# A decoder block with routed experts on one core: the early tiles of the first expert hold tokens of four groups instead of six, and the narrowest up products have 224 columns instead of 256

## What is computed

```python
N, E, K, CF = 4096, 8, 2, 1.25
cap = int(N * K * CF / E)                       # 1280
logits = x @ Wg.T
top_v, top_i = jax.lax.top_k(logits, K)
gates = jax.nn.softmax(top_v, axis=-1)
...
keep = pos_f < cap                              # pos: the token's place in its expert's queue
exp_batches = zeros((E, cap, d)).at[flat_e, pos_safe].set(x[tok], mode='drop')
h = einsum('ecd,edf->ecf', exp_batches, W1)     # 512 -> 2 x 1024: "up"
inp, gate = split(h, 2, axis=-1)
h = gelu(inp, approximate=False) * gate
exp_out = einsum('eci,eid->ecd', h, W2)         # 1024 -> 512: "down"
out = segment_sum(gates * gathered rows of exp_out, tok)
```

## Time and profile before

| what | us |
|---|---|
| median of 3 runs (lowest to highest) | 1474.22 (1474.14 to 1477.27) |
| the profiled execution's own time | 1474.55 |
| its span, first to last instruction | 1472.8 |
| PE busy in the span | 1430.7 |
| first up product of the early tiles | at 472.37 |
| first up product of the first expert's later tokens | at 512.43 |

### The profile page before, as it was taken

The page is one execution under the profiler, slowest core; times in us unless marked ns, Lnnn a source line. Parts: engine busy times, 40 slices in busy tenths (PEclk is TensorE's granted clock), DMA queues, the critical chain, the costliest instruction groups (busy, mean ns, idle before and its releaser), DMA issues.

```text
span 1472.8 us, 22222 instructions
## 1 busy us (share of the span) xinstructions
PE 1430.7 (97%) x7508; PEld 1210.8 (82%) x7509; DVE 640.8 (44%) x1379; ACT 591.7 (40%) x1018; POOL 374.8 (25%) x365
## 2 busy tenths in 40 slices
PE   7999999989989999999999999999999999999997
PEld 5768887778876888889889888899889888898886
DVE  7535666657777563123524421166223420253111
ACT  5534554258776552223424421255323321252212
POOL 3302232137666412203202211121301111021111
PEclk9999999999998999999999999999999999999999
DMA  6331223218658764204505421156504412052112
GB/s 206 60 64 30 86 87 58 86 33 209 172 133 221 176 186 108 42 2 85 151 34 123 107 64 34 21 157 189 132 7 118 103 57 43 7 152 54 21 36 28
DMA packets 82854, 135.64 MB, mean 92 GB/s; under 512 B 33234, under 2 KB 33362, under 8 KB 81780
## 3 DMA queue, kind: packets, MB, share of 16 engines
q1 hardware_dynamic: 65428, 97.68, 23.2%
q0 software_dynamic: 17376, 37.30, 13.8%
HBM read 94.41 MB, written 40.55 MB: 92 GB/s over the span
## 4 chain that ended last, share of the span: by engine, by line
PE 90%; DVE 3%; ACT 2%; issue 2%; DMA 1%; POOL 1%; SPq 0%; POOLq 0%; DVEq 0%; ACTq 0%
PE pg L1050 16%; PE pg L1052 16%; PE pg L1051 16%; PE pj L1050 10%; PE pj L1051 10%; PE pj L1052 10%; PE pj L1289 2%; PE pg L1317 2%; PE pt L1458 2%; PE pg L1255 2%; PE pt L1276 1%; PE pt L1071 1%; DMA out_rows<-ost,etab 1%; DVE kf L1582 1%; PE pt L1201 1%
## 5 line engine op out<-in xcount | busy, mean ns | idle before, releaser
L1050 PE MATMUL pg<-xe_hi,w_hi 128*128 128x512 f32 (+2 forms) x1152 | 401.7, 349 | 3.0 <-DVE xe_lo L1534 1.9
L1051 PE MATMUL pg<-xe_lo,w_hi 128*128 128x512 f32 (+2 forms) x1152 | 401.1, 348 | 0.0
L1052 PE MATMUL pg<-xe_hi,w_lo 128*128 128x512 f32 (+2 forms) x1152 | 401.0, 348 | 0.0
L1994 DVE TENSOR_TENSOR hp<-gl,pg 128x512 f32<-128x512 f32 x136 | 93.5, 688 | 569.9 <-ACT gl L1021 569.9
L728 POOL DMA_INDIRECT out_rows<-ost,etab x62 | 99.6, 1606 | 721.7 <-ACT ost L1005 359.0
L1021 ACT ACTIVATE gl<-pg 128x512 f32<-128x512 f32 x136 | 81.3, 598 | 410.9 <-PE pg L1052 410.9
L1050 PEld LDWEIGHTS pg<-xe_hi,w_hi 128*128 128x128 f32 x1152 | 218.5, 190 | 29.0 <-issue 2.8
L1051 PEld LDWEIGHTS pg<-xe_lo,w_hi 128*128 128x128 f32 x1152 | 218.5, 190 | 25.0
L1052 PEld LDWEIGHTS pg<-xe_hi,w_lo 128*128 128x128 f32 x1152 | 218.5, 190 | 25.0
L1050 PE MATMUL pj<-w_hi,hg_hi 128*128 128x512 f32 x448 | 177.0, 395 | 0.0
L1052 PE MATMUL pj<-w_hi,hg_lo 128*128 128x512 f32 x448 | 174.5, 389 | 0.0
(11 more groups left out here) (250 smaller groups left out, 1992.8 us busy)
## 6 DMA issues: line engine op xcount, KB each, us to landing
stage<-w SPq DMA_DIRECT2D x96, 512.0 KB, 4.1
xr<-x SPq DMA_DIRECT2D x8, 1024.0 KB, 10.6
out_rows<-xr SPq DMA_DIRECT2D x8, 1024.0 KB, 7.3
x_rows<-xn SPq DMA_DIRECT2D x8, 1024.0 KB, 7.1
x_in<-x SPq DMA_DIRECT2D x7, 1024.0 KB, 6.0
x_rows<-zrow POOLq DMA_DIRECT2D x1, 2304.0 KB, 15.7
late_xT<-xT_hi SPq DMA_DIRECT2D x2, 1024.0 KB, 3.9
late_xT<-xT_lo SPq DMA_DIRECT2D x2, 1024.0 KB, 6.0
```

What stands on the lines that cost most here:

```text
L1050: nc.tensor.matmul(o, lh, rh, start=start, stop=False)
L1051: nc.tensor.matmul(o, lh, rl, start=False, stop=False)
L1052: return nc.tensor.matmul(o, ll, rh, start=False, stop=stop)
L1994: v.tensor_tensor(hp[j % 2][:], gl[j % 2][:], pg[:, 2 + j % 2, :], ALU.mult).then_inc(s_hp, 1)
```

## The change

There are two parts. The first moves the early tiles: they hold tokens of the first four groups (SOON = GROUPS - 4), are gathered at the end of POOL's period 4 instead of 6, and are turned, copied and split into high and low in period 5 (SOON_TURNED) instead of 7. They get tiles of their own (`soon_xe_hi`, `soon_xe_lo`) for it, and a turn that takes a PSUM bank afterwards waits for the early rows to have left it. The weight pieces on SP's queue keep their places (periods 6 and 7). The zeros that are stored under `x_rows` begin at group 4, 17 tiles of rows instead of 9. The second part changes the widths of the up products: from 2, 3 and 4 tiles (256, 384 and 512 columns, by `left` up to 256, up to 384, and above) to the list UP_WIDTHS of 224, 384 and 512, of which the narrowest that holds `left` is taken.

```diff
+UP_WIDTHS = [2 * P - 32, 3 * P, 4 * P]
...
-SOON, SOON_TILES = GROUPS - 2, 2
+SOON, SOON_TILES = GROUPS - 4, 2
+SOON_TURNED = SOON + 1
...
+    soon_xe_hi = alias("soon_xe_hi", [P, KC, SOON_SLOTS], F32R, one_at + 8192 * 7)
+    soon_xe_lo = alias("soon_xe_lo", [P, KC, SOON_SLOTS], F32R, one_at + 8192 * 7 + 4096)
...
-                if g == SOON:
+                if g == GROUPS - 2:
                     first_pieces(range(STG, STG + 2))
...
+                if g == SOON_TURNED:
+                    rows_hi(0, range(SOON_TILES), soon_xe_hi)
                 if g == GROUPS - 1:
-                    rows_hi(0, range(SOON_TILES))
                     for s in range(2, STG):
                         split(0, s)
...
             def bank(k):
 
                 if last[k]:
                     pe.wait_ge(s_btev, last[k])
+                if soon_turned[k]:
+                    pe.wait_ge(s_xelo, soon_turned[k])
...
-                if not more_groups:
+                if g == SOON_TURNED:
                     turn_soon()
-                    positions(g)
+                positions(g)
                 if more_groups:
-                    positions(g)
                     scores(g + 1, at_x1)
...
-                    with pe.If(left < 2 * P + 1):
-                        up(2)
-                    with pe.Else():
-                        with pe.If(left > 3 * P):
-                            up(4)
+                    def up_narrowest(widths):
+
+                        if len(widths) == 1:
+                            up(widths[0])
+                            return
+                        half = len(widths) // 2
+                        with pe.If(left < widths[half - 1] + 1):
+                            up_narrowest(widths[:half])
                         with pe.Else():
-                            up(3)
+                            up_narrowest(widths[half:])
+
+                    up_narrowest(UP_WIDTHS)
...
                 if more_groups:
                     cross_out(g)
                     positions_out(g)
+                    if g == SOON_TURNED:
+                        rows_lo_of(0, range(SOON_TILES), soon_xe_lo, soon_xe_hi)
                     score_stats(g + 1)
...
                 else:
                     cross_out(g)
-                    rows_lo_of(0, range(SOON_TILES))
                     positions_out(g)
```

More of the change, by code:

```diff
@@ L896, in normalise3, with rows_hi @@
                                  scale=rstd[1][:, i:i + 1]).then_inc(s_xn3, 1)
-            def rows_hi(first, tiles):
+            def rows_hi(first, tiles, to):
                 for i in tiles:
                     act.wait_ge(s_xet, first + i + 1)
-                    a.activation(xe_hi[:, :, i * P:(i + 1) * P],
+                    a.activation(to[:, :, i * P:(i + 1) * P],
                                  pt[i % 2][:].rearrange("p (k t) -> p k t", k=KC), ACT.Copy).then_inc(s_xehi, 1)
@@ L981, in _ @@
                 if i == 0:
-                    rows_hi(SOON_TILES, range(CHUNKS[0]))
+                    rows_hi(SOON_TILES, range(CHUNKS[0]), xe_hi)
             act.wait_ge(s_meta, 1)
@@ L1258, in attend @@
                     ins.then_inc(s_o, 1)
-            nt, last = [0], [0, 0]
+            nt, last, soon_turned = [0], [0, 0], [0, 0]
             def bank(k):
@@ L1341, in turn_soon @@
                     ins.then_inc(s_xet, 1)
+                    soon_turned[i] = i + 1
             attend(0, range(2))
@@ L1402, in _ @@
                         ins = three(pg[:, 2 * half + j % 2, 0:SOON_SLOTS], w1_hi[:, j, k, m], w1_lo[:, j, k, m],
-                                    xe_hi[:, k, 0:SOON_SLOTS], xe_lo[:, k, 0:SOON_SLOTS], k == 0, k == KC - 1)
+                                    soon_xe_hi[:, k, :], soon_xe_lo[:, k, :], k == 0, k == KC - 1)
                 ins.then_inc(s_h, 1)
@@ L1436, in _, with up @@
                     following = pe.snap(first + 2 + (c < 2) * 2, min_val=2, max_val=EX * ET + 14)
-                    def up(tiles):
-                        w = tiles * P
+                    def up(w):
                         pe.wait_ge(s_xelo, following)
@@ L1878, in pack_tokens, with rows_lo_of @@
                 v.tensor_tensor(gate[:, :, 1, 1], ge[:], gate[:, :, 0, 1], ALU.mult).then_inc(s_dest, 1)
-            def rows_lo_of(first, tiles):
+            def rows_lo_of(first, tiles, lo, hi):
                 for i in tiles:
                     dve.wait_ge(s_xehi, first + i + 1)
-                    low(xe_lo[:, :, i * P:(i + 1) * P], pt[i % 2][:].rearrange("p (k t) -> p k t", k=KC),
-                        xe_hi[:, :, i * P:(i + 1) * P]).then_inc(s_xelo, 1)
+                    low(lo[:, :, i * P:(i + 1) * P], pt[i % 2][:].rearrange("p (k t) -> p k t", k=KC),
+                        hi[:, :, i * P:(i + 1) * P]).then_inc(s_xelo, 1)
             def w_parts(s):
@@ L1966, in _ @@
                     counts()
-            rows_lo_of(SOON_TILES, range(CHUNKS[0]))
+            rows_lo_of(SOON_TILES, range(CHUNKS[0]), xe_lo, xe_hi)
             dve.wait_ge(s_meta, 1)
```

## The result

The changed kernel takes 1492.85 us (median of 4 executions, 1487.38 to 1500.81) against 1474.18 us before: a ratio of 1.0127, 95% interval 1.0071 to 1.0182, or +18.7 us (+10.5 to +26.8). The profiled execution took 1488.75 us, 14.2 us above that of before. Two of the four executions, at 1497 and 1501 us, had a mean granted clock of 0.986 to 0.987 instead of 0.995, and the profile is of one of the other two.

A forecast was written before the change was run, and what follows sets the result against it. PE was taken as the bound, busy 1430.7 of 1472.8 us. Terms +20.5 - 3.8 + 1.7 - 3.0 = +15.4 on the profiled 1474.55 gave 1489.95, from the median 1489.6; given as 1489.8 us, range 1484.5 to 1495.5.

The forecast's parts named there:

- Widths, wider: Experts' loop: two full chunks of 256 tokens go from 256 to 384 columns, unhidden, +20.5 us.
- The rival that they don't widen: Experts' loop: the two full chunks have `left` at most 224, so all five narrow; 1466.9 us, chance 0.02.
- Widths, narrower: Experts' loop: three chunks go from 256 to 224 columns at 0.1134 us a product, -3.8 us, bounds 0 and -7.7.
- Columns alone: Rival, experts' loop: a 224-column product costs 0.1066 us, so three narrow chunks save 7.7 us; 1486 us, chance 0.12.
- the rival that small products slow down: Experts' loop: columns cost more below 256 columns, 576 products 54 us more; some 1536 us, chance 0.02.
- the 3.8 us of the floor: Saving forecast for three 224-column chunks, with a product's price held at a floor of 0.1134 us.
- Period 5: Early tiles' turn ahead of group 6's scores: PE waits 0.75 us, transposes take 1.03, all passed on, +1.7 us.
- POOL's margin: Period 5: POOL's last query addition ends at 436.7 to 437.2, PE wants it at 437.1; taken as 0, bound 1 us.
- Last period: Early tiles' transposes and a wait go, early up products start 2.9 us sooner; -3.0 us, bounds -1.5 and -4.1.
- the wait of 1.06 us: Last period: PE's wait for low parts of early rows ahead of the early up products, claimed to go.
- the hold that the text had named without a price: Last period: weight pieces, loaded by SP as DVE finishes earlier ones, can hold a later step; no size given.
- Sum: Whole kernel: the four terms give +15.4 us, forecast time 1489.8 us, chance 0.73.

The follow-up runs named there:

- e4: The changed kernel with five up widths (160, 224, 256, 384, 512) instead of three: 1694.88 us, ratio 1.1465 to the kernel before.
- e1: Only the move of the early tiles, put on the kernel before, with widths 256, 384 and 512 kept: 1476.69 us, ratio 1.0007.
- e10: The changed kernel with the pause ahead of group 6's exponentials filled by six products of unused result: 1490.32 us, ratio 1.0115 to the kernel before.

## Why the prediction came out

**Widths, wider.** Right: +20.54 us, forecast +20.5. Two chunks of exactly 256 tokens ran 384 columns, at the price of the earlier trace rows, with no wait that hid any of it. The rival that they don't widen fell.

**Widths, narrower.** Right in kind, but the term was a little small: -4.8 us, forecast -3.8, since a product of 224 columns costs 0.1116 us and not the 0.1134 that was taken from the scores. Columns alone fell, by the 21.43 us and by e4's 160 columns. So did the rival that small products slow down; its 1536 us should have been 1540 by its own sum, since the 3.8 us of the floor were not given back.

**Period 5.** Right: the turn took 1.78 us ahead of the scores, forecast 1.7, with a wait of 0.71 for ACT's copy, and all of it went through the pause into the time. POOL's margin was wider than the text had it. Its next table write came at 419.29 and not at 421.5, and its last addition for the queries ended at 434.99 and not at 436.7 to 437.2, where PE comes to them at 436.65:

```profile
433.72 1.27 POOL L614 TENSOR_TENSOR qT<-fe,frl 128x512 f32<-128x512 f32 x1
```

What the step lacked is the clock: the stretch at 1.2 GHz at the pause became 3.4 us longer, and from the scores to the next period another 0.75 us were lost.

**Last period.** From 2.02 us late to 1.42 sooner is 3.44 gained, forecast 3.0. The size is right partly by luck. Of the forecast 2.9 us up to the early products, only the transposes' 1.7 came as told: the wait of 1.06 us did not go, but became one of 1.00 us for the last residual rows. What made up for it is the clock, which was full here and saved 1.9 us on the values, where the text had left it at 1.2 GHz at that point. Behind the start the full clock won nothing more on balance, since the waits for gelu products grew from 1.2 to 2.6 us. Only 0.64 of these lie behind a late piece of weights, the hold that the text had named without a price; 1.66 lie behind the gates' differences. The early products started at 470.74 and the down products at 497.12, forecast 471.2 and 497.2.

**Sum.** +14.2 us in the profiled execution, forecast +15.4. The median is 4 us above that because two of four executions were long, and no step allowed for executions of different length. Going by e1 and e10, the long ones come from the clock behind the pause; with the pause filled the changed kernel takes 1490.3 us. Why the clock comes back after 3.4, 6.8 or 23.9 us (the last two in kernels that are the same up to there), and why it falls in some last periods and not in others, is open.

## What to carry to other kernels

List the amounts of work that occur before you choose the sizes of a case distinction: a size that is hit exactly, as 256 was twice, costs a whole step when the limit moves below it. Measure also where a smaller size stops paying: here a product of 160 columns cost what one of 224 does. A further case would have cured it on paper, but the cases of an unrolled loop share the room for its code: look at the packets on the instruction queue before and after adding one, since even a case that never ran cost 37 us here. When executions spread, look for a pause of PE and the granted clock behind it, and put useful work into the pause before filling it with anything else: here the turn with three or four products without use made the move 2 us faster than the kernel before, and six products without use made it 1.5 us faster.

## What was not expected of the hardware

- PE's code in this loop is free up to a length, and beyond it packets come again in later passes: 30 packets with three copies of 192 products (also with a quarter more), 66 with a fourth that never ran, 54 with a fourth that ran, 167 with five, and 1695 us.
- A float32r product costs 0.1116 us at 224 columns and 0.1120 at 160, but 0.1200 at 256: a floor below, a line above.
- With a pause of 3.9 to 4.1 us came 3.4 to 23.9 us at 1.2 GHz, up to a whole period of the kernel; six products without use in the pause removed that in three profiles of three, but not the 10.2 us in the last period.
